# A routed mixture of experts, reordered from phases into a pipeline over token groups

## The reference, cut to what matters

```
def moe_apply(x, combine, dispatch, W, b):
    disp = jnp.einsum('sec,sd->ecd', dispatch, x)
    h = jnp.einsum('ecd,edf->ecf', disp, W) + b[:, None, :]
    return jnp.einsum('sec,ecf->sf', combine, h)
def per_group(xf, lw, lb):
    combine, dispatch = top2_dispatch(xf, Wg, C)
    h = moe_apply(xf, combine, dispatch, W1, b1)
    h = jax.nn.relu(layer_norm(h, lw, lb))
    return moe_apply(h, combine, dispatch, W2, b2)
```

## Time and profile before

| | us |
|---|---|
| Median of three runs | 512.89 |
| Lowest, highest | 511.42, 515.46 |
| The profiled execution | 513.19 |
| Its span in the trace | 511.5 |
| PE, DVE, ACT, POOL busy | 363.7, 284.9, 189.4, 120.6 |

### The profile page before, as it was taken

One profiled execution on the slowest core, in us unless ns is written; L12 is line 12 of the kernel. 1 busy time (PEld: TensorE's weight loads), 2 busy tenths in 40 slices (PEclk: granted clock), 3 DMA queues, 4 the chain that ended last, 5 costly groups with the idle time before them and its releaser, 6 DMA issues.

```text
span 511.5 us, 5686 instructions
## 1 busy us (share of the span) xinstructions
PE 363.7 (71%) x2003; PEld 217.2 (42%) x2003; DVE 284.9 (56%) x678; ACT 189.4 (37%) x299; POOL 120.6 (24%) x151
## 2 busy tenths in 40 slices
PE   2987404990458999999986998887299636789800
PEld 1667303990223333333233855447153204569700
DVE  5235400341559888888417864446883199941255
ACT  2222101320231377767874867362223213431100
POOL 2000275005623711111100000000300279610172
PEclk9998555996558799999999999978589856889955
DMA  5790013112265650000130000199906443101123
GB/s 104 206 326 11 11 51 100 32 33 60 52 153 157 165 139 7 3 2 2 41 126 0 1 1 1 41 382 312 258 26 212 143 144 103 42 1 45 47 52 68
DMA packets 33888, 46.76 MB, mean 91 GB/s; under 512 B 4937, under 2 KB 19568, under 8 KB 33604
## 3 DMA queue, kind: packets, MB, share of 16 engines
q1 hardware_dynamic: 31044, 39.09, 26.3%
q0 software_dynamic: 2816, 7.31, 5.2%
HBM read 34.00 MB, written 12.22 MB: 90 GB/s over the span
## 4 chain that ended last, share of the span: by engine, by line
PE 57%; DVE 18%; POOL 8%; issue 6%; DMA 5%; ACT 5%; SPq 0%; POOLq 0%; DVEq 0%; ACTq 0%
PE ps L1211 8%; PE ps L1408 6%; PE ps L1379 5%; POOL R L481 5%; PE ps L1396 5%; PE ps L1664 4%; PE ps L1597 3%; PE ps L1326 3%; PE ps L1338 3%; DVE mcol L1020 2%; PE ps L1621 2%; PE ps L1500 2%; POOL disp_d L476 2%; PE ps L1548 2%; PE ps L1588 2%
## 5 line engine op out<-in xcount | busy, mean ns | idle before, releaser
L1020 DVE TENSOR_REDUCE mcol<-ps 128x1 f32<-128x512 f32 x128 | 80.7, 686 | 7.6 <-PE ps L1379 7.3
L649 ACT ACTIVATE R<-ps 128x1024 f32<-128x1024 f32 x64 | 62.5, 1021 | 26.8 <-PE ps L1396 25.9
L1211 PE MATMUL ps<-ident,R 128*77 128x128 f32 (+1 forms) x216 | 32.4, 289 | 27.4 <-DMA R<-disp_d 24.6
L481 POOL DMA_INDIRECT R<-y_d,grow x32 | 30.4, 949 | 77.4 <-DMA y_d<-R 68.2
L1379 PE MATMUL ps<-R 72*128 72x512 bf16 x128 | 47.7, 405 | 0.9
L1211 PEld LDWEIGHTS ps<-ident,R 128*77 128x77 f32 (+1 forms) x216 | 25.3, 151 | 44.5 <-DMA R<-disp_d 25.0
L1396 PE MATMUL ps<-R 75*128 75x512 bf16 x128 | 37.8, 382 | 0.3 <-ACT R L649 0.2
L1621 PE MATMUL ps<-R 128*128 128x264 bf16 x192 | 27.5, 314 | 11.2 <-POOL R L544 10.5
L1408 PE MATMUL ps<-R,vaug 128*9 128x512 f32 x256 | 33.5, 595 | 0.6 <-ACT R L649 0.6
L1211 PE MATMUL ps<-ident,xn 128*128 128x128 f32 x48 | 12.5, 400 | 29.6 <-issue 18.0
L1621 PEld LDWEIGHTS ps<-R 128*128 128x128 bf16 x192 | 21.0, 111 | 19.5 <-issue 13.1
(11 more groups left out here) (288 smaller groups left out, 683.6 us busy)
## 6 DMA issues: line engine op xcount, KB each, us to landing
R<-in_L_ffn_W_dram SPq DMA_DIRECT2D x1, 6144.0 KB, 19.7
h_d<-R SPq DMA_DIRECT2D x24, 176.0 KB
q_d<-R SPq DMA_DIRECT2D x24, 96.0 KB, 2.1
R<-k_d SPq DMA_DIRECT2D x24, 96.0 KB
R<-q_d SPq DMA_DIRECT2D x8, 288.0 KB
R<-in_L_ffn_w_dram SPq DMA_DIRECT2D x1, 2048.0 KB, 11.7
y_d<-R SPq DMA_DIRECT2D x24, 44.0 KB
disp_d<-zeros SPq DMA_DIRECT2D x1, 1024.0 KB, 5.7
```

Source lines behind the costliest of these rows:

```text
L481: g.indirect_dma_start(into[:, t, k, :], None, src, bass.IndirectOffsetOnAxis(ap=index[:, k, t:t + 1], axis=0)).then_inc(gathered[t], 16)
L649: s.activation(probs[idx % 4], ps[:, 2 * (idx % 2):2 * (idx % 2) + 2, :].rearrange("p b t -> p (b t)"), ACT.Exp, scale=QK_SCALE).then_inc( ...
L1020: v.tensor_reduce(mcol[:, u, col:col + 1], bank(ring_bank("row", n)), AX.X, ALU.max).then_inc(s1_max, 1)
L1211: return m.transpose(dst, src, ident[0:k, 0:k])
```

## The change

The first products go by token group and by quad of experts. A quad is four matmuls of 32 slot columns each (22 of the expert, 10 that belong to the next or are padding), into partitions 0, 32, 64, 96 of one bank. There are 6 quads a group, 24 in all. Their rows go to four memory tensors, one a group, in blocks of 128, through a ring of six buffers. POOL gathers a group's rows as soon as that group's two halves are stored. Three banks (2, 3, 4) serve the quads, and a table gives the bank of each bias product. PE's queue is: dispatch of groups 0 and 1, quads 0 to 5, dispatch of 2 and 3, transposes of `comb`, quads 6 to 11, bias products 0 to 2, quads 12 to 23, a wait for the last three copies, bias products 3 to 5, then the dispatch of hidden group 0, bias 6, group 1, bias 7, groups 2 and 3. ACT copies 21 of the quads and DVE three (7, 9, 11).

The affine weights of the hidden norm are loaded as 32 more rows of `vrow` and transposed into columns of `vcol`; they are applied as scale and bias of the activation that evacuates a chunk. The broadcast loads of them go. Mean and variance are applied by ACT (`hid_norm`), two activations per tile, one to bf16 and one to fp32. DVE now does both subtractions that POOL did, and `hparts` is six deep. All evacuations of the last group are on ACT. The diff, cut to its core:

```diff
+QUADS = E1 // 4
+DVE_QUADS = (7, 9, 11)
+W1_BANKS = (2, 3, 4)
+BIAS_BANK = (5, 1, 0, 2, 3, 4, 5, 2)
...
-            for e in range(E1):
-                sp.wait_ge(h1_dve if e % 2 else h1_act, e // 2 + 1)
-                sp.dma_start(h1_d[M1 * e:M1 * (e + 1), :], ring[e % 4]).then_inc(ring_dma[e % 4], 16)
+            for i in range(NG * QUADS):
+                gr, s = i // QUADS, i % QUADS
+                wait_quad_copied(sp, i)
+                if gr >= 2 and s % 3 == 0:
+                    wait_half_stored(sp, gr - 2, s // 3)
+                sp.dma_start(h1_d[gr][P * s:P * (s + 1), :], ring[s]).then_inc(h1_wr[2 * (gr % 2) + s // 3], 16)
...
+            for gr in range(NG):
+                for half in range(2):
+                    wait_half_stored(pool, gr, half)
+                for q in (2 * gr, 2 * gr + 1):
+                    t = paired[q]
+                    if q == 3:
+                        pool.wait_ge(slot_onehot, T)
+                    if q >= 4:
+                        pool.wait_ge(hvar, q - 3)
+                    for k in range(2):
+                        g.indirect_dma_start(got1[q % 4][:, k, :], None, h1_d[gr],
+                                             bass.IndirectOffsetOnAxis(ap=growh[:, k, t:t + 1], axis=0)).then_inc(gathered[t], 16)
...
+            def copy_quad(i):
+                gr, slot = i // QUADS, i % QUADS
+                act.wait_ge(h1_mm, i + 1)
+                if gr >= 1:
+                    wait_half_stored(act, gr - 1, slot // 3)
+                s.copy(ring[slot], bank(W1_BANKS[i % 3])).then_inc(h1_act, 1)
+            def hid_norm(q):
+                act.wait_ge(hid_ready, q + 1)
+                if q >= 6:
+                    act.wait_ge(hdisp_mm, 4 * ((q - 6) // 2 + 1))
+                for dst in (hparts[q % 6][:, 0, :], hsum[q % 4]):
+                    ins = s.activation(dst, hsum[q % 4], ACT.Identity, bias=rstds[:, 1, q:q + 1], scale=rstd[:, q:q + 1])
+                ins.then_inc(hid_p1, 1)
+            def hid_middle(q):
+                act.wait_ge(hid_r1, q + 1)
+                s.copy(hparts[q % 6][:, 1, :], hsum[q % 4]).then_inc(hid_p2, 1)
...
-                             ACT.Relu).then_inc(hid1T_ready, 1)
+                             ps[:, bk:bk + 2, 0:CG // 2].rearrange("p a (e c) -> p a e c", c=C1), ACT.Relu,
+                             bias=vcol[:, V_HB + c:V_HB + c + 1], scale=vcol[:, V_HW + c:V_HW + c + 1]).then_inc(hid1T_ready, 1)
+            evac_slots1(0)
+            evac_slots1(1)
+            for i in range(QUADS):
+                copy_quad(i)
+            evac_slots1(2)
+            evac_slots1(3)
+            for b in range(B):
+                act.wait_ge(comb_tp, b + 1)
+                s.copy(combT[:, b * SEQ:(b + 1) * SEQ], ps[0:E1, b, :]).then_inc(combT_ready, 1)
+            for i in (6, 8, 10, 12, 13, 14):
+                copy_quad(i)
+            hid_std(0)
+            copy_quad(15)
+            hid_norm(0)
+            copy_quad(16)
+            copy_quad(17)
+            for q in (1, 2):
+                hid_middle(q - 1)
+                hid_std(q)
+                copy_quad(15 + 3 * q)
+                hid_norm(q)
+                copy_quad(16 + 3 * q)
+                copy_quad(17 + 3 * q)
+            for q in range(3, T):
+                hid_middle(q - 1)
+                hid_std(q)
+                hid_norm(q)
+                if q >= 4:
+                    evac_hidden(2 * (q - 4))
+                    evac_hidden(2 * (q - 4) + 1)
+            hid_middle(T - 1)
+            for c in range(2 * (T - 4), 4 * NG):
+                evac_hidden(c)
...
+            for i in DVE_QUADS:
+                gr, slot = i // QUADS, i % QUADS
+                dve.wait_ge(h1_mm, i + 1)
+                wait_half_stored(dve, gr - 1, slot // 3)
+                v.tensor_copy(ring[slot], bank(W1_BANKS[i % 3])).then_inc(h1_dve, 1)
...
                     dve.wait_ge(gathered[t], 64)
                     dve.wait_ge(hb_mm, q + 1)
+                    me.link(v.scalar_tensor_tensor(out=hsum[q % 4], in0=got1[q % 4][:, 0, :], scalar=g1[:, 0, t:t + 1],
+                                                   in1=bank(BIAS_BANK[q]), op0=ALU.mult, op1=ALU.add))
                     second = me.step(v.scalar_tensor_tensor(out=hsum[q % 4], in0=got1[q % 4][:, 1, :], scalar=g1[:, 1, t:t + 1],
                                                             in1=hsum[q % 4], op0=ALU.mult, op1=ALU.add))
                 if q >= 1:
+                    dve.wait_ge(hid_p1, u + 1)
+                    v.tensor_tensor(hsum[u % 4], hsum[u % 4], hparts[u % 6][:, 0, :], ALU.subtract).then_inc(hid_r1, 1)
                 if q < T:
                     me.wait(second)
+                    me.link(v.bn_stats(st6[:, q, :], hsum[q % 4]))
                     me.link(v.bn_aggr(mv[:, q, :], st6[:, q, :]))
                     v.tensor_scalar(tmp8b[:, q:q + 1], mv[:, q, 1:2], MOE_EPS, None, ALU.add).then_inc(hvar, 1)
+                if q >= 1:
+                    dve.wait_ge(hid_p2, u + 1)
+                    v.tensor_tensor(hparts[u % 6][:, 2, :], hsum[u % 4], hparts[u % 6][:, 1, :], ALU.subtract).then_inc(hid_p3, 1)
+                if q < T:
+                    dve.wait_ge(hstd, q + 1)
+                    me.link(v.reciprocal(rstd[:, q:q + 1], tmp8[:, q:q + 1]))
+                    v.tensor_scalar(rstds[:, 1, q:q + 1], mv[:, q, 0:1], rstd[:, q:q + 1], -1.0,
+                                    ALU.mult, ALU.mult).then_inc(hid_ready, 1)
...
+            def first_product(gr):
+                pe.wait_ge(slots1T_ready, gr + 1)
+                for i in range(QUADS * gr, QUADS * (gr + 1)):
+                    if i >= 3:
+                        wait_quad_copied(pe, i - 3)
+                    for j in range(4):
+                        e = 4 * (i % QUADS) + j
+                        ins = m.matmul(ps[32 * j:32 * j + 32, W1_BANKS[i % 3], :], slots1T[:, gr, C1 * e:C1 * e + 32], W1[:, e, :],
+                                       start=True, stop=True)
+                    ins.then_inc(h1_mm, 1)
+            def hidden_bias(q):
+                t = paired[q]
+                if q >= 6:
+                    pe.wait_ge(hvar, BIAS_BANK[0:q].index(BIAS_BANK[q]) + 1)
+                m.matmul(bank(BIAS_BANK[q]), combT[:, t * P:(t + 1) * P], b1_1[:, :], start=True, stop=True).then_inc(hb_mm, 1)
...
+            first_product(2)
+            first_product(3)
+            for i in range(NG * QUADS - 3, NG * QUADS):
+                wait_quad_copied(pe, i)
+            hidden_bias(3)
+            hidden_bias(4)
+            hidden_bias(5)
...
             for gr in range(NG - 1):
-                if gr + 2 < NG:
-                    hidden_bias(2 * gr + 4)
-                    hidden_bias(2 * gr + 5)
-                pe.wait_ge(hid_p2, 2 * gr + 2)
                 pe.wait_ge(hid_p3, 2 * gr + 2)
                 for f in range(4):
                     c = 4 * gr + f
...
                     ins.then_inc(hdisp_mm, 1)
+                if gr < 2:
+                    hidden_bias(6 + gr)
```

More of the change, by code:

```diff
@@ L280, in flamingo_kernel, with wait_quad_copied, wait_half_stored @@
             sem("ob_mm"), sem("out_ready"), sem("out_done"))
-        N_VEC, N_BIAS, N_WX = 12, 9, 10
+        N_VEC, N_BIAS, N_WX = 14, 9, 10
         paired = [gr + TB * b for gr in range(NG) for b in range(B)]
+        act_quads = [i for i in range(NG * QUADS) if i not in DVE_QUADS]
+        def wait_quad_copied(eng, i):
+            if i in DVE_QUADS:
+                eng.wait_ge(h1_dve, DVE_QUADS.index(i) + 1)
+            else:
+                eng.wait_ge(h1_act, act_quads.index(i) + 1)
+        def wait_half_stored(eng, gr, half):
+            eng.wait_ge(h1_wr[2 * (gr % 2) + half], 16 * (QUADS // 2) * (gr // 2 + 1))
         chunk_bank = lambda c: 6 * (c % 2) if c < 4 * (NG - 1) else (0, 6, 2, 4)[c % 4]
@@ L740, in evac_hidden @@
                 s.activation(hid1T[f].rearrange("p (a e m) -> p a e m", a=2, m=M1)[:, :, :, C1 * gr:C1 * (gr + 1)],
-                             ps[:, bk:bk + 2, 0:CG // 2].rearrange("p a (e c) -> p a e c", c=C1),
-                             ACT.Relu).then_inc(hid1T_ready, 1)
[L744 to L749, removed]
-                    s.copy(hparts[u % 4][:, 0, :], hsum[u % 4]).then_inc(hid_p1, 1)
-                if q < T:
-                    act.wait_ge(hvar, q + 1)
-                    s.activation(tmp8[:, q:q + 1], tmp8b[:, q:q + 1], ACT.Sqrt).then_inc(hstd, 1)
-                if 1 <= q < T:
-                    act.wait_ge(hid_r1, u + 1)
-                    s.copy(hparts[u % 4][:, 1, :], hsum[u % 4]).then_inc(hid_p2, 1)
-                if q >= 3:
-                    evac_hidden(2 * (q - 3))
-                    evac_hidden(2 * (q - 3) + 1)
@@ L1580, in _, with dispatch @@
             pe.wait_ge(y_parts, 4)
-            for gr in range(NG):
+            def dispatch(gr):
                 if gr >= 2:
@@ L1591, in _ @@
                     ins.then_inc(disp_mm, 1)
```

(19 more changed lines are left out.)

142 lines of the change are left out of this document (38 added, 104 removed).

## The result

| us | before | changed |
|---|---|---|
| Median of 20 runs each, side by side | 512.92 | 516.31 |
| Lowest, highest | 511.24, 516.41 | 511.00, 520.18 |
| Ratio | | 1.0048, interval 1.0024 to 1.0071 |
| The profiled execution, its span | 513.19, 511.5 | 513.73, 512.0 |

The changed kernel is half a per cent slower: forecast 517.3, measured 516.31. The changed kernel's single runs lie wider apart than those of the kernel before, 9 us against 5, and the one that was profiled is among the shorter.

What follows compares the result with a forecast made beforehand. The bound was taken as a string of phases, each waiting for the one before, up to the second products. Their start moves from 460.3 to 464.7, +4.4: 517.6 profiled, less 0.3 gives 517.3 us; range 506.5 to 524.

Steps and rivals of the forecast that it cites:

- stalls 1, 2, 3: DVE's loop waiting for PE's bias products before q=3, q=6 and q=7: 4.3, 3.7 and 8.2 us late.
- Products per quad: First products on PE: 1.0 us a quad (0.86 to 1.05), 24 us for what cost 20.7 before.
- the rival of 571: First products on PE: 32-column groups don't overlap, a quad costs 3.45 us, some 54 more, 571; chance 0.02.
- Copies out of PSUM: Quad copies on ACT, 0.59 each against a quad of 1.0, don't set the pace until quad 12.
- The pair: Two ACT activations per tile, with scale and bias from memory: 1.24 to 1.56 us, taken 1.45.
- Evacuation: ACT's evacuation of a chunk with ReLU: 0.61 us before, 0.80 at most with two operands, taken 0.65.
- The body: One turn of DVE's loop over token tiles: 4.2 us (3.9 with overlaps, 4.5 with waits).
- Stall 2: Before q=6: bias 6 stands behind group 0's four chunks in PE's queue, so DVE gets it 3.7 us late.
- The stage's sum: All terms from the common origin 375.6 put the second products at 464.7 instead of 460.3, +4.4 us.
- The clock stays up: PE's bursts in the loop keep 2.4 GHz; stalls and end lose 6.4 us, time 510.9; chance 0.2.
- DMA landings hidden: Row stores and gathers ahead of DVE's loop: 0 to 2 us more on landings, hidden by a 2 to 4 us lead.
- the long ends: Pair 1.6, evacuations 0.8, 5 us at half clock, quads 1.05: second products at 471.9, time 524.2; chance 0.13.

Runs made afterwards that it cites:

- first profile: The changed kernel's profiled execution from the side-by-side measurement against the kernel before: 513.73 us, span 512.0.
- second profile: The changed kernel measured once more, no edit: 518.2 us over 12 runs, ratio 1.0061 to the kernel before; its profiled run took 519.35.
- the fold alone: Kernel before with only the affine part folded into the evacuations; phases stay, POOL keeps its subtractions: 511.52 us, ratio 0.9966 to the kernel before.

## Why the prediction was right

Times from the first dispatch of the stage, so that the start of the stage drops out:

| us | predicted | first profile | second profile |
|---|---|---|---|
| hid_ready(0) | 29.2 | 27.5 | 29.5 |
| q=3 starts | 42.7 | 40.4 | 41.8 |
| q=6 starts | 59.3 | 55.0 | 58.1 |
| q=7 starts | 71.7 | 67.0 | 71.3 |
| second products | 94.3 | 89.2 | 93.4 |
| stalls 1, 2, 3 | 4.3, 3.7, 8.2 | 4.5, 1.9, 8.0 | 3.9, 3.5, 9.1 |

- *The mechanism* is shown: the three stalls sit where they were put, with the bias product as releaser. Stalls 2 and 3 go when their two products alone are moved; stall 1 falls from 4.52 to 1.08 when its three are.
- *Products per quad*: 1.0 taken, 0.88 measured, near the low end. Column groups of 32 do overlap; the rival of 571 is refuted. Over the fifteen quads ahead of the root of tile 0 that is 1.8, and hid_ready(0) came 1.7 early in the first profile; in the second the clock's fall over quads 12 and 13 took it back.
- *Copies out of PSUM*: up to quad 17 PE never waited for a copy; ahead of quads 18, 19 and 22 it waited 2.3 in all (L1620), since ACT had root and pairs between its copies, as the prediction had it.
- *The pair*: 1.45 taken; measured 812 and 799 ns, 1.52 from start to end. *Evacuation*: 0.65 taken, 0.79 measured, four in 2.85 instead of 2.6. The upper end, from L564, was the nearer row: what cost time was the two operands from memory, not the source.
- *The body*: 4.2 was right; 4.47 where ACT ends each turn.
- *Stall 2* was mis-sized for the first profile: 3.7 came with a burst whose first four microseconds were at half clock, and chunks 2 and 3 ran at full clock in 2.87. In the second they took 4.54, and the stall was 3.52.
- *The stage's sum*, 94.3, fits the second profile to 0.9 and the first only to 5.1. That the forecast fits the median to 1.0 is in part luck: the median lies between the two, and two errors have opposite signs. The sum took the second products as untouched, though they lose the clock soon after their start, +1.7 in both profiles, and it had the quads 0.12 too long.
- *The clock stays up*, at 510.9, did not come: 0.50 at 412 and 0.70 at 431 in the first profile. Its price of 6.4 is neither shown nor refuted: matmuls in the gaps bought 3.3 us in the changed kernel without reaching chunks 2 and 3, and in their profile, in which the clock fell over quads 12 and 13 as in the second profile here, the stage is 89.7 instead of 93.4.
- *DMA landings hidden* was true in both profiles of the changed kernel, but by little. The row store took up to 5.42 and the gather of tile 2 up to 5.94 from issue to landing, against 3.1 and 5.2 in the sum. In the three experiments in which the root came as early as in the first profile, or earlier, DVE waited 1.40 to 1.75 for the gather of tile 2, which none of their edits touches: the lead of 2 to 4 us was not there. With stall 1 shortened it waited for that of tile 4 too, 0.39 and 0.86.
- *Slips in the sums*, without weight: from 471.9 the long ends give 524.5 and not 524.2; turns of 4.2 give 421.5 and 425.7 for hid_ready(4) and (5); and the "seconds of idleness" are 7.35 us.

What stays open: why the clock falls over quads 12 and 13 in some executions. It did in five of the nine profiles that have this part of the change, and in these the stage also began later (370.8 to 374.4 against 369.5 to 369.9), though the work ahead of it is the same. What sets the landing of tile 2's gather, and what the clock would be worth if it never fell, is open too.

## What to carry to other kernels

When phases are turned into a pipeline, look through each in-order queue for small operations that open another engine's work and stand behind long work that waits on that engine in turn: here two matmuls of about a microsecond cost the whole gain. Price idle time by what waits for it: of the four idle stretches of DVE the one at the first root could be taken out without any gain, as the next things in line, the same copies and a gather, filled its place. Judge the merits of dropping a pass with the other engines' traffic beside it, in the version in which it will run.

## What the runs showed of the chip

- The granted clock fell to 0.50 in the middle of work, over quads 12 and 13, with PE busy for 2.00 of 2 us. A fall is not only a matter of idle time ahead of it.
- The second products lasted 22.87 or 22.88 in four profiles and 21.21 in two, all six with the same gap of 2.26 us ahead of them. After gaps of 2.42 (the fold alone), 1.57 and 1.24 (the kernel before) they took 21.18, 21.21 and 21.18. The length of the gap does not decide it. Where the clock falls, it does so in the middle of work: 1.00 in the first half microsecond of the products, 0.50 from a microsecond after their start.
- A DVE pass with one tensor input grows from 0.53 to 1.67 beside a POOL subtraction of 1.16, and ends 0.29 after it.
